# A three-layer graph network on one core: blocks of one kind, three layers in one stage, tables made elsewhere

## The reference

```
loops = arange(N); src, dst = [src, loops], [dst, loops]
dinv = rsqrt(in-degree); norm = dinv[src] * dinv[dst]
for l in 0, 1, 2:
    h = x @ W[l].T
    agg = segment_sum(h[src] * norm, dst) + b[l]
    xn = (agg - mean(agg)) * rsqrt(var(agg) + eps)     # over all 10,000 nodes
    x' = relu(gamma[l] * xn + beta[l])
x = layernorm(x_in + x'_3)
x = layernorm(x + message_network(x, src, dst, edge_attr_20, edge_weight, edge_attr_3))
```

## Time and profile before

| | us |
|---|---|
| median of 3 runs (1854.6 to 1856.04) | 1854.98 |
| the profiled execution, its own time | 1854.7 |
| its span in the trace | 1853.0 |
| sort stage, ends at | 187 |
| first product to last eviction of layer 0 | 221.6 to 536.9 |
| the same, layer 1 | 574.7 to 860.8 |
| the same, layer 2 | 908 to 1161.4 |
| `finish_gcn` to its last store | 1161 to 1497 |
| `messages` and `touched` | to the end |

### The profile page before, as it was taken

The page is one execution under the profiler, slowest core; times in us unless marked ns, Lnnn a source line. Parts: engine busy times, 40 slices in busy tenths (PEclk is TensorE's granted clock), DMA queues, the critical chain, the costliest instruction groups (busy, mean ns, idle before and its releaser), DMA issues. The chain is left out here.

```text
span 1853.0 us, 27588 instructions
## 1 busy us (share of the span) xinstructions
PE 1396.9 (75%) x8180; PEld 1204.7 (65%) x8180; DVE 1206.3 (65%) x3308; ACT 982.5 (53%) x1960; POOL 1048.5 (57%) x1095
## 2 busy tenths in 40 slices
PE   4669599999968999996699999353333239999833
PEld 4558488888856888885588888242232128888722
DVE  6575466666637777763699997464444239999865
ACT  3743144444425777762566664385656634444476
POOL 4773757777534787774423320577777744333236
PEclk8995699999987999998799999566655569999955
DMA  2000556666545766753555552888786532233112
GB/s 58 2 2 1 151 196 222 218 223 220 192 161 205 260 250 241 252 200 143 212 180 220 210 185 107 257 279 271 256 267 234 200 118 84 88 90 91 52 62 112
DMA packets 98920, 313.66 MB, mean 169 GB/s; under 512 B 34576, under 2 KB 36064, under 8 KB 98802
## 3 DMA queue, kind: packets, MB, share of 16 engines
q0 software_dynamic: 62720, 183.99, 29.5%
q1 hardware_dynamic: 36082, 128.24, 19.6%
HBM read 161.18 MB, written 156.39 MB: 171 GB/s over the span
## 5 line engine op out<-in xcount | busy, mean ns | idle before, releaser
L851 PE MATMUL ps_b<-yhi,whi 128*128 128x500 f32 x960 | 390.3, 407 | 8.6 <-DVE ylo L718 8.6
L851 PE MATMUL ps_b<-yhi,wlo 128*128 128x500 f32 x960 | 375.2, 391 | 0.0
L851 PE MATMUL ps_b<-ylo,whi 128*128 128x500 f32 x960 | 374.9, 390 | 0.0
L795 ACT COPY aggT<-ps_b 128x500 f32<-128x500 f32 x240 | 137.9, 574 | 347.1 <-PE ps_b L851 347.1
L747 DVE BATCH_NORM_STATS2 stat<-aggT 128x6 f32<-128x500 f32 x240 | 163.2, 680 | 200.4 <-ACT aggT L795 198.3
L635 POOL DMA_INDIRECT rows<-rows_out,node_at x160 | 187.0, 1169 | 118.3 <-ACT rows_out L800 82.7
L1068 PE MATMUL fin_ps_x<-ident,fin_X 128*127 128x128 f32 (+1 forms) x320 | 75.4, 405 | 176.9 <-DVE fin_xr L1000 163.4
L851 PEld LDWEIGHTS ps_b<-yhi,whi 128*128 128x128 f32 x960 | 182.5, 190 | 40.1 <-DVE ylo L718 9.1
L851 PEld LDWEIGHTS ps_b<-yhi,wlo 128*128 128x128 f32 x960 | 181.4, 189 | 37.8
L851 PEld LDWEIGHTS ps_b<-ylo,whi 128*128 128x128 f32 x960 | 182.4, 190 | 30.8
L1068 PEld LDWEIGHTS fin_ps_x<-ident,fin_X 128*127 128x127 f32 (+1 forms) x320 | 65.8, 298 | 192.8 <-DVE fin_xr L1000 169.2
(11 more groups left out here) (344 smaller groups left out, 3319.8 us busy)
## 6 DMA issues: line engine op xcount, KB each, us to landing
...
rows<-rows_out,node_at POOLq DMA_INDIRECT x160, 3.1
...
others<-ord_nodeid,ord_place_node POOLq DMA_INDIRECT x80, 2.1
R<-in_x,node_at POOLq DMA_INDIRECT x80, 3.6
G<-rows,srci POOLq DMA_INDIRECT x80, 5.3
```

The costliest lines, as they stand in the source:

```text
L795: nc.scalar.copy(f.aggT[t % 2][:, j, :], f.ps_b[j % 2][:, 0:COLS]).then_inc(x["copied"], 1)
L851: o = nc.tensor.matmul(f.ps_b[j % 2][:, 0:COLS], w[:, c, j * P:(j + 1) * P], y[b % 2][:, c, :], start=(c == 0 and i == 0), stop=(c == C - ...
```

## The change

Blocks are of one kind: ten with four edge tiles (508 columns) and ten with four plain tiles (492), in the order `"PP" + "EP"*8 + "EE"`. The three layers are one stage, `graph_layers`, without barriers between; each layer begins with two plain blocks, whose columns need no gathered row. `X` of the next layer's first blocks is loaded while the old one ends, `bn_aggr` follows each chunk's last statistics, and `trow` is made after the first product. Weights of layers 0 and 1 are split in turns 4 to 11 of the sort loop, through one PSUM bank; those of layer 2 in turns 2 to 7 of layer 1. The two rows that the 160 matmuls spread go through DRAM: SP stores them and loads them with a broadcast (four DMAs, 5.2 MB) into `sel` and `own_row`; DVE makes `cont`, `flag` and `sel` four tiles at a time in layer 0 (`build`). All 40 id gathers (`place`) are in layer 0, where 24 were before. Layer 0's node rows also go to DRAM by SP (`x_rows`, 20.5 MB), and `finish_gcn` loads them again by one SP DMA for each block in place of four POOL gathers; half of its `out` tiles are made by DVE.

```diff
@@ Machine @@
+        self.COLS = 4 * max(self.EPT, self.PPT)
+        self.NE = self.ET // 4
+        self.kinds = "PP" + "EP" * (self.NE - 2) + "EE"
     def tile(self, b, j):
-        if j < 2:
-            return 2 * b + j, self.EPT, j * self.EPT
-        return self.ET + 2 * b + j - 2, self.PPT, 2 * self.EPT + (j - 2) * self.PPT
+        n = self.lanes(b)
+        return 4 * self.nth(b) + j + (0 if self.kinds[b] == "E" else self.ET), n, j * n
@@ order_edges, SP @@
+            sp.wait_ge(colsT_out, 2)
+            sp.dma_start(a.match_rows.rearrange("(t p) -> t p", p=P), s.colT[:, 0, :]).then_inc(rows_out, 16)
+            sp.dma_start(a.own_rows.rearrange("(t p) -> t p", p=m.EPT), s.colT[:, 1, 0:m.EPT]).then_inc(rows_out, 16)
+            sp.wait_ge(rows_out, 32)
+            for i, (lo, hi) in enumerate(k.parts):
+                sp.dma_start(k.sel[:, lo * P:hi * P], a.match_rows[lo * P:hi * P].rearrange("(o n) -> o n", o=1)
+                             .to_broadcast([P, (hi - lo) * P])).then_inc(k.match_in[i], 16)
@@ order_edges, DVE @@
             for t in range(ET + 1):
                 for i in range(2):
                     if t < ET - 1:
                         advance(i, t)
                     if t >= 1:
                         looks(i, t - 1)
+                if 0 <= t - W_FROM < 2 * C:
+                    n = t - W_FROM
+                    dve.wait_ge(whi, n + 1)
+                    nc.vector.tensor_tensor(k.wlo[n // C][:, n % C, :], s.ps_cnt[:], k.whi[n // C][:, n % C, :].bitcast(F32),
+                                            ALU.subtract).then_inc(wlo, 1)
@@ order_edges, PE (ACT waits for wt, n + 1, and copies ps_cnt to whi) @@
+                if 0 <= t - W_FROM < 2 * C:
+                    n = t - W_FROM
+                    pe.wait_ge(signed, C * (n // C + 1))
+                    ge(pe, wlo, n)
+                    for c in range(C):
+                        w = nc.tensor.transpose(s.ps_cnt[:, c * P:(c + 1) * P],
+                                                s.rawW[n // C][:, c, (n % C) * P:(n % C + 1) * P], k.ident[:])
+                    w.then_inc(wt, 1)
@@ graph_layers, DVE @@
+            def build(o):
...
+                dve.wait_ge(k.match_in[part], 16)
...
+                nc.vector.tensor_tensor(k.cont[:, lo:hi, :], keys[:, lo:hi, :],
+                                        keys[:, lo - 1:hi - 1, P - 1:P].to_broadcast([P, hi - lo, P]), ALU.is_equal).then_inc(x["cont"], 1)
+                for i in range(4 * o, 4 * o + 4):
+                    nc.vector.tensor_scalar(k.sel[:, i * P:(i + 1) * P], k.sel[:, i * P:(i + 1) * P], k.srt[:, i:i + 1],
+                                            k.weight[:, i:i + 1], ALU.is_equal, ALU.mult).then_inc(x["tabled"], 1)
@@ graph_layers, POOL @@
+            def body(layer, t):
+                ahead = 3 if layer == 0 else 4
+                for j in range(4):
+                    if layer == 0 and runs(t + 3):
+                        own(t + 3, j)
+                    if m.edges(t + ahead):
+                        gather(layer, 4 * m.nth(t + ahead) + j, a.x if layer == 0 else table[layer - 1])
+                    if layer == 0 and m.edges(t + 5):
+                        place(t + 5, j)
+                    if layer < L - 1 and runs(t - 1):
+                        leave(layer, t - 1, j)
@@ graph_layers, ACT @@
+            def body(layer, t):
+                if layer > 0 and m.edges(t + 2) and t > 0:
+                    sources(layer, t + 2)
+                if layer > 0 and runs(t + 2):
+                    relu(layer, t + 2)
+                for j in range(4):
+                    if runs(t + 1):
+                        if m.plain(t + 1) and j < 2:
+                            high(layer, t + 1, 2 * j)
+                            high(layer, t + 1, 2 * j + 1)
...
+                    if runs(t):
+                        act.wait_ge(x["product"], C * g + j + 1)
...
+                        nc.scalar.copy(f.aggT[t % 2][:, j, 0:cols(t)], f.ps_b[j % 2][:, 0:cols(t)]).then_inc(x["copied"], 1)
@@ graph_layers, SP @@
+                if layer == 0 and runs(t + 2):
+                    for j in range(4):
+                        n = 4 * (t + 2) + j
+                        sp.wait_ge(r_in[n % 8], 16 * (n // 8 + 1))
+                        sp.dma_start(x_rows[t + 2, :, j, :], f.R[n % 8][:]).then_inc(r_out[n % 8], 16)
@@ finish_gcn, SP, then POOL, DVE and ACT @@
             for b in range(3):
+                sp.dma_start(f.xr[b][:], x_rows[b]).then_inc(x_in[b], 16)
...
-                        pool.indirect_dma_start(f.xr[n % 16][:], None, a.x,
-                                                bass.IndirectOffsetOnAxis(ap=k.node_at[:, m.tile(t + 4, j)[0]:m.tile(t + 4, j)[0] + 1], axis=0),
...
+                    for j in range(2):
+                        nc.vector.tensor_scalar(f.out[n % 8][:], f.x2[n % 8][:], f.rstd2[t % 2][:, j:j + 1], None,
+                                                ALU.mult).then_inc(x["edge_out"], 1)
...
-                    for j in range(4):
+                    for j in range(2, 4):
                         nc.scalar.activation(f.out[n % 8][:], f.x2[n % 8][:], ACT.Copy,
```

More of the change, by code:

```diff
@@ L579, in layer_stage @@
-    put = [m.sem(f"{tag}_put{i}") for i in range(4)]
-    sent = [m.sem(f"{tag}_sent{i}") for i in range(2)]
-    whi, wlo = k.whi[wset], k.wlo[wset]
-    makes_w = layer >= 2
-    edges = slice(0, 2 * EPT)
-    def each_turn(body):
-        for t in range(-5, NB + 1):
-            body(t)
+             "hi", "lo", "product", "copied", "counted", "back", "rows", "zero", "tabled", "cont")
+    x = {n: m.sem(f"gcn_{n}") for n in names}
+    g_in = [m.sem(f"gcn_g_in{i}") for i in range(4)]
+    h_in = [m.sem(f"gcn_h_in{i}") for i in range(8)]
@@ new lines, in body @@
+                if layer == 0 and m.edges(t + 3):
+                    build(m.nth(t + 3))
+                if t == 0:
+                    if layer > 0:
+                        shifts(layer, 2)
+                    for j in range(4):
+                        merge(layer, j)
+                if layer > 0 and t > 0 and m.edges(t + 3):
+                    shifts(layer, t + 3)
+            for spare in f.R + f.rows:
+                nc.vector.memset(spare[:], 0.0).then_inc(x["zero"], 1)
+            nc.vector.memset(k.cont[:, 0, :], 0.0).then_inc(x["cont"], 1)
@@ L830, in _ @@
+            act.wait_ge(x["zero"], 12)
+            for layer in range(L):
+                if layer > 0:
+                    act.wait_ge(x["var"], C * layer)
+                    nc.scalar.activation(s.std[:], s.mv[:, :, 1], ACT.Sqrt, bias=k.eps[:, 0:1]).then_inc(x["root"], 1)
+                    act.wait_ge(x["factor"], 2 * layer)
+                for t in range(-5, NB + 1):
+                    body(layer, t)
         @block.tensor
         def _(pe):
-            parts = [(whi, f.yhi), (whi, f.ylo), (wlo, f.yhi)]
@@ L921, in runs, with cols @@
         return 0 <= b < NB
+    def cols(b):
+        return 4 * m.lanes(b)
     with nc.Block() as block:
@@ L1573, in build @@
         k = Bag()
-        k.ident, k.ones, k.before, k.after, k.count = (m.sb(n, [P, P]) for n in ("ident", "ones", "before", "after", "count"))
-        k.identb = m.sb("identb", [P, P], BF16)
+        k.ident, k.ones = (m.sb(n, [P, P]) for n in ("ident", "ones"))
         k.part, k.eps = m.sb("part", [P, 1]), m.sb("eps", [P, 1])
```

669 lines of the change are left out of this document (337 added, 332 removed).

## The result

The changed kernel took 1789.16 us (median of 4, 1787.06 to 1789.84) against 1854.79 of the kernel before: the ratio is 0.9643, 95% interval 0.9627 to 0.966. The range of 1722 to 1792 held it, near its upper end; the forecast's own range of 1735 to 1768 did not. Rival C (1782, the layers lose more) came nearest by the number, though not by the mechanism that it named; and the finish was even faster than rival B had it, which made good part of the loss.

A forecast was written before the change was run, and what follows sets the result against it. PE bounds the layers' steady parts, POOL's issues the finish; PE idles between. Terms -24 +2 +4 -20 -29.5 +5 +14 -55 = -103.5 us from 1854.7 gave 1751, given as 1750; range 1722 to 1792.

The forecast's parts named there:

- Rival C: Bunched edge work costs the layers more: layer 0 +16, layer 2 +11, layer 1 +4; 1782 us, chance 0.28.
- rival B: Finish falls to POOL's bound, 10.4 us a block, and ACT's head in edge turns is hidden; 1725 us, chance 0.17.
- the second transition: Layer 1's last eviction to layer 2's first: an 18.5 us ACT chain replaces a 52.7 us gap; with merges, -29.5 us.
- the weight turns' serial chain: Sort stage: eight weight turns add a second chain in series, 2.5 us each; with ACT's sign scalings +23 us.
- the head of the source relus: Layer 2: ACT's work, source relus included, before an edge turn's first eviction makes PE wait 1.7 us in eight turns.
- Turn 0's merges: First turn after each transition: merges behind four shifts and relus cost 4 us, and trow's matmul 0.5.
- ACT's queue ahead of the first eviction: Layer 2's edge turns: this queue takes 9.0 us where PE wants the bank after 7.3; +14 us (0 to 25).
- The queue is full but just not over: Layer 0: POOL's 24 indirect DMAs take 31.0 to 32.5 us a pair against PE's 31.5; +4 us (0 to 20).
- rival E: POOL's queue in layer 0 holds back PE in every pair; slower, 1888 us at 1.9 an issue, chance 0.04.
- So the DMA engines come next: Finish: DMA, 11.6 us busy a block, sets the pace after POOL falls to 10.4; 11.5 a block, -55 us.
- The first transition: Layer 0's last eviction to layer 1's first: an 18.5 us ACT chain replaces a 43.0 us gap; with merges, -20 us.
- the start: Sort stage and layer 0's fill: first product at 197.5 us instead of 221.64; -24 us.

The follow-up runs named there:

- e1: Changed kernel with GpSimd's multiplication of X by own_row in layers 1 and 2 left out (edge columns' numbers then wrong): 1748.04 us.
- e2: Changed kernel with ScalarE taking the relu of X ahead of the four source relus instead of behind them: 1753.8 us.
- e5: Changed kernel with GpSimd's multiplication by own_row in layers 1 and 2 cut into four instructions at the same place: 1760.64 us.
- e3: Changed kernel with each layer 0 join right behind its merge instead of all four at the start of the next turn: 1774.38 us.
- e6: Changed kernel with the finish's input rows fetched again by four GpSimd gathers a block instead of one SP load: 1875.63 us.

## Why the prediction was right, and where it was not

**Right.** The sign; the second transition to half a microsecond, each piece of ScalarE's chain as listed; the weight turns' serial chain (3.85 forecast, 3.6 in a plain turn; +23 for all eight forecast, +26 seen) and that it was not overlapped; the end of the sort stage (170, first memset at 171.6); the head of the source relus (1.7 a pair forecast, 1.5 in e1, where nothing else is in the way). Turn 0's merges were named but priced too low (4.5 forecast, 6.8 and 6.6 seen). That the total still fell into the range is in part luck: layers 0 and 2 lost 55 us beyond their terms, and the finish gained 29 beyond its own.

**Layer 2, the step that failed.** "In layer 2 ACT's queue ahead of the first eviction is: ..." priced one engine's queue and took the durations of all others from rows in which they ran alone. The change also made two GpSimd instructions of 2.0 and 2.4 us into one of 4.5, and moved it, behind four source relus, to where VectorE has its `ylo`. e1 puts the hold at 39.7 us, e2 shows that it goes by the place, e5 that it goes by the instruction's length. I had no term for it. The trace of before had the sign of it: the joins' group in its page has a mean of 959 ns, and the timeline has two joins that begin beside the multiplication:

```profile
1014.28 3.23 DVE L710 TENSOR_TENSOR X<-X,V 128x508 f32<-128x508 f32 x2
```

```profile
1013.97 2.39 POOL L650 TENSOR_TENSOR X<-X,own_row 128x1016 f32<-128x1016 f32 x1
```

3.23 us for two, where two such joins took 1.28 in layer 0 of the same trace (the row at 367.42 below). It is so in nearly every turn of layer 2, and was hidden there: PE was busy 247.27 of 247.31 us. The rule I cited and then gave little weight (the Trainium skill, SBUF — State Buffer, SBUF: two separate sides) has this very case beside its two-port one: whichever of a VectorE operation with two SBUF inputs and a GpSimd operation that reads SBUF starts first has the port pair for its whole instruction. The traces agree, with 5.17 us against 1.39, and in e2 the multiplication, begun under the shifts, took 5.00 instead of 4.54. I weighed the rule only for `build`, against GpSimd, and not the other way round.

**Layer 0, a term mis-sized.** "The queue is full but just not over: +4 (0 to 20 ...)". The queue was as full as said; the stretch came not from `build` (1.07 us beside it) but from four joins in a row, 1.3 to 2.5 us on one issue a pair. +19.1 in place of +6; e3 takes 13.8 of it back and leaves 5.3. Here a reading was wrong too: "The longest id gather took 1.33 us" is true of those at L238 alone. Layer 0 of the same trace has one of 2.12 us, beside two joins:

```profile
367.45 2.12 POOL L620 DMA_INDIRECT node_at<-others,free_row  x1 [0.30 <-issue]
```

```profile
367.42 1.28 DVE L710 TENSOR_TENSOR X<-X,V 128x508 f32<-128x508 f32 x2
```

A `G` and an `R` gather beside such joins took 1.87 and 1.59. These rows named the operation at fault, and with them rival E's "the longest of its kind 1.33 + 0.30" falls as well.

**The finish, a term mis-sized the other way.** "So the DMA engines come next ... I take 11.5". A busy share times a period was taken for the time that the bytes need. They went at 381 GB/s where they had gone at 251, and GpSimd's 8 issues set the pace, as rival B had it. e6 shows the share back at 0.75 with the gathers. Two other parts of the term were off, and partly cancel. From the first `fin_x` to block 19's it took 181.1 us, 42 less than the forecast's 223.5 (19 x 11.5 + 5) and 21.5 less than B's pace gives with the same 5; ScalarE's lead over GpSimd's queue, seen before too (264.9 us where 19 x 15.66 is 297.5), was not in the sum. And the logarithms were to end 10 us after block 19 instead of 23; they ended 23.1 after it (1428.27), as before, 13 worse than forecast. So -84.4 stands near rival B's -76 in part by chance.

**The first transition and the start** are off by 4.5 and 5: a `rows_out` copy that waited for a store to land; VectorE's memsets, for which GpSimd's first issue waited until 178.98, and node rows for which PE waited.

**Not settled.** Layer 1 lost 14.9 us; 6.8 are turn 0, 3.6 the multiplication in its last turns (e1), and the other 4.5 lie for the most part in turns 1 to 7, which also make layer 2's weights. No experiment took these apart.
